# A gated two-layer cross-attention kernel on one core: first queries and scores pulled in front of the last projections, the pair work of each turn put together and shifted, another order at the end

## What is computed

```python
x = x + tanh(g_xattn[0]) * cosine_attention(layernorm(x), ctx)        # layer 0
x = x + tanh(g_ffn[0])   * ternary_ffn(layernorm(x))                  # layer 0
q = layer_norm(layernorm(x), g_norm) @ Wq                             # layer 1, attention
k, v = split(ctx @ Wkv)                                               # plus a null key and value
p = softmax(q @ k.T / 8)                                              # per head, 128 x 129
y = layer_norm((p @ v) @ Wout, g_out)
x = x + tanh(g_xattn[1]) * y
x = x + tanh(g_ffn[1])   * int8_ffn(layernorm(x))                     # layer 1, one global scale
```

## Time and profile before

| what | us |
|---|---|
| median of 3 runs | 317.86 (317.69 to 320.22) |
| the profiled execution | 317.06 |
| its span in the trace | 315.2 |
| busy: PE, DVE, ACT, POOL | 288.3, 249.9, 236.7, 158.0 |

### The profile page before, as it was taken

The page is one execution under the profiler, slowest core; times in us unless marked ns, Lnnn a source line. Parts: engine busy times, 40 slices in busy tenths (PEclk is TensorE's granted clock), DMA queues, the critical chain, the costliest instruction groups (busy, mean ns, idle before and its releaser), DMA issues.

```text
span 315.2 us, 7749 instructions
## 1 busy us (share of the span) xinstructions
PE 288.3 (91%) x2618; PEld 238.6 (76%) x2618; DVE 249.9 (79%) x730; ACT 236.7 (75%) x811; POOL 158.0 (50%) x225
## 2 busy tenths in 40 slices
PE   6788999999999898999999999999999997977775
PEld 6567768687776676899998998989989896842475
DVE  3798999999977436766878878898788988858875
ACT  3777696969899667899887889878898886429290
POOL 2124617252442104655587896868857585453200
PEclk9999999999999999999999999999999999999979
DMA  5741010001020000000000000000000000000004
GB/s 157 195 120 25 1 27 1 1 2 67 3 67 1 2 0 0 2 3 3 2 3 0 2 2 2 2 2 4 0 3 2 1 2 3 2 0 0 1 2 133
DMA packets 11478, 6.67 MB, mean 21 GB/s; under 512 B 3824, under 2 KB 10992, under 8 KB 11440
## 3 DMA queue, kind: packets, MB, share of 16 engines
q1 hardware_dynamic: 10560, 5.99, 6.7%
q10 hardware_dynamic: 880, 0.20, 0.3%
HBM read 5.14 MB, written 1.05 MB: 20 GB/s over the span
## 4 chain that ended last, share of the span: by engine, by line
PE 46%; DVE 22%; ACT 11%; POOL 9%; issue 7%; DMA 3%; SPq 2%; DVEq 0%; ACTq 0%; POOLq 0%
PE psum L1074 9%; DVE rmx L2029 6%; PE psum L1078 6%; PE psum L1202 5%; PE psum L1080 5%; PE psum L1079 5%; PE psum L1523 4%; ACT work L1005 4%; PE psum L1539 4%; POOL work L584 3%; PE psum L1648 3%; DVE work L2022 2%; DMA KT<-in_L_ffn_w_down 2%; DVE hgm L2228 2%; DVE den L2044 2%
## 5 line engine op out<-in xcount | busy, mean ns | idle before, releaser
L1005 ACT ACTIVATE work<-psum,nmx 128x128 f32<-128x128 f32 x208 | 74.2, 408 | 0.0
L584 POOL TENSOR_TENSOR work<-work,rden 128x512 f32<-128x512 f32 x51 | 53.1, 1043 | 40.9 <-DVE rden L2048 40.9
L1005 ACT ACTIVATION_READ_ACCUMULATOR work<-psum,nmx 128x1 f32 x208 | 51.6, 248 | 0.0
L1074 PE MATMUL psum<-ident,work 128*128 128x128 f32 (+2 forms) x328 | 47.1, 276 | 4.6 <-POOL work L584 2.1
L1074 PEld LDWEIGHTS psum<-ident,work 128*128 128x128 f32 (+2 forms) x328 | 36.8, 141 | 11.3 <-issue 2.7
L2029 DVE TENSOR_REDUCE rmx<-psum 128x8 f32<-128x1024 f32 x32 | 38.5, 1204 | 4.5 <-PE psum L1202 4.5
L1078 PE MATMUL psum<-split 128*128 128x256 f32 (+1 forms) x96 | 36.7, 383 | 3.0 <-ACT work L993 1.5
L1202 PE MATMUL psum<-KT,work 64*128 64x128 f32 x512 | 35.9, 283 | 2.0 <-ACT work L1005 1.2
L1202 PEld LDWEIGHTS psum<-KT,work 64*128 64x128 f32 x512 | 31.4, 187 | 6.5 <-issue 4.3
L2044 DVE SCALAR_TENSOR_TENSOR den<-null_exp,masked,key_sum 128x4 f32<-128x4 f32 x64 | 19.1, 299 | 18.9 <-ACT work L1005 13.0
L1080 PE MATMUL psum<-split 128*128 128x256 f32 (+1 forms) x96 | 30.6, 319 | 0.0
(11 more groups left out here) (216 smaller groups left out, 767.8 us busy)
## 6 DMA issues: line engine op xcount, KB each, us to landing
KT<-in_L_xattn_Wkv SPq DMA_DIRECT2D x2, 384.0 KB, 4.5
X<-in_x SPq DMA_DIRECT2D x1, 768.0 KB, 5.6
out_x<-X SPq DMA_DIRECT2D x3, 256.0 KB, 2.6
work<-in_ctx SPq DMA_DIRECT2D x3, 192.0 KB, 2.5
work<-in_L_xattn_Wq SPq DMA_DIRECT2D x1, 512.0 KB, 3.7
work<-in_L_xattn_Wout SPq DMA_DIRECT2D x1, 512.0 KB, 4.0
X<-in_x SPq DMA_DIRECT2D x1, 256.0 KB, 3.5
KT<-in_L_ffn_w_gate SPq DMA_DIRECT2D x1, 256.0 KB, 5.4
```

Source lines behind the costliest of these rows:

```text
L584: pool.tensor_tensor(sx_, sx_, bcast(rden[n % 2][:, :], S), ALU.mult).then_inc(p_ready.sem, 1)
L1005: ins = act.activation(Sx[n % 5][:, j, :], bank[2 * (r % 2) + j % 2][:, at * S:(at + 1) * S], ACT.Exp, bias=nmx[r % 2][:, col:col + 1], ac ...
L1074: return pe.transpose(dst, src, ident[0:m, 0:m])
```

## The change

- **Seam.** `q_first(0)` goes in front of `kv(60)` and `q_first(1)` behind `kv(61)`, into banks 5 and 6, with waits on those banks alone. `scores(0)` and `scores(1)` come right behind `kv(63)`; they now wait for the copies of chunks 0 to 62 and of one query chunk. `next_transposes(3)`, `q_first(2)` and `q_first(3)` follow them. On ACT the copies of the first two query chunks stand among those of the chunks 60 to 63, and those of the last two in turn 1, each behind the exponents of a unit.
- **Turns, DVE.** Both pair works stand between the second and the third denominator. The maxima of round 2M stand in front of the fourth denominator.
- **Turns, when pair work is done.** Statistics of the sum one round later (m = 4t + 14), aggregation and rstd one round later (15), normalised rows one round later (16 and 17), their maximum at 18. On POOL rstd of the sum thereby moves from the first half of an odd turn to its end, behind `y_affine`.
- **Drain.** DVE does the maxima of round 31 first and its copies in another order. POOL normalises all 64 units and does its pair work 32 behind unit 63. The steps of pairs 4 and 5 that had been done in turn 16 or before now stand among the last ones.
- 18 idle-filling matmuls in place of 22, and other banks for them.

```diff
-        X_STATS_AT, X_AGGR_AT, RSTD_X_AT, XN4_AT, GM_AT = 13, 14, 14, 15, 17
+        X_STATS_AT, X_AGGR_AT, RSTD_X_AT, XN4_AT, GM_AT = 14, 15, 15, 16, 18
...
             for M in range(NT + 1):
                 for k in range(2):
                     for n in range(4 * (M - 1) + 2 * k, 4 * (M - 1) + 2 * k + 2):
-                        if 0 <= n < NS - 1:
+                        if n >= 0:
                             normalise(n)
-                    pair_work(2 * M + k)
+                    if M < NT:
+                        pair_work(2 * M + k)
+            pair_work(2 * NT)
             rstd_x(NPAIR - 3)
...
-            for k in range(58, 64):
+            for k in range(58, 61):
                 kv_evac(k)
-            q_evac(0, bank[0])
-            q_evac(1, bank[1])
+            q_evac(0, bank[5])
+            kv_evac(61)
+            kv_evac(62)
+            q_evac(1, bank[6])
+            kv_evac(63)
             x_evac(3)
-            q_evac(2, bank[0])
-            q_evac(3, bank[1])
...
                     if q_round(2 * M + k):
                         q_round_evac(*q_round(2 * M + k))
+                    elif M == 1:
+                        q_evac(2 + k, bank[5 + k])
...
                 if hg == 0:
                     pe.wait_ge(wq_split.sem, wq_split.at(2))
                     pe.wait_ge(xs_ready.sem, xs_ready.at(1))
-                    pe.wait_ge(kv_out.sem, kv_out.at(0, NG))
-                    pe.wait_ge(cos_step.sem, cos_step.at(1, NG - 1))
-                    pe.wait_ge(third_in.sem, third_in.at(third(("u", NG - 1)) + 1))
+                if hg < 2:
+                    pe.wait_ge(hqT_ready.sem, hqT_ready.at(3 + hg, NG - 1))
...
                 if n == 0:
-                    pe.wait_ge(q_out.sem, q_out.at(4))
+                    pe.wait_ge(kv_out.sem, kv_out.at(NKV - 1, NG - 1))
+                    pe.wait_ge(cos_step.sem, cos_step.at(1, NG - 1))
...
             down(3, 3)
-            for k in range(60, 64):
-                kv(k)
-            q_first(0, bank[0])
-            q_first(1, bank[1])
-            next_transposes(3)
-            q_first(2, bank[0])
-            q_first(3, bank[1])
+            q_first(0, bank[5])
+            kv(60)
+            kv(61)
+            q_first(1, bank[6])
+            kv(62)
+            kv(63)
             scores(0)
             scores(1)
+            next_transposes(3)
+            q_first(2, bank[5])
+            q_first(3, bank[6])
...
-                    keep_clock_long(bank[5], 2)
+                    keep_clock_long(bank[4], 2)
...
-                    keep_clock_long(bank[5], 22)
+                    keep_clock_long(bank[4], 18)
...
             for M in range(NT + 1):
                 old, new = 4 * (M - 2), 4 * (M - 1)
+                if M == NT:
+                    maxima(2 * M - 1)
                 if old >= 0:
                     p_evac(old)
                     p_evac(old + 1)
+                if 0 < M < NT:
+                    maxima(2 * M - 1)
                 if new >= 0:
-                    maxima(2 * M - 1)
                     denominators(new)
                 if old >= 0:
                     p_evac(old + 2)
+                if M == NT:
+                    denominators(new + 1)
+                if old >= 0:
                     p_evac(old + 3)
-                if new >= 0:
+                if 0 < M < NT:
                     denominators(new + 1)
                 if M == NT:
                     p_evac(NS - 4)
-                pair_work(2 * M)
+                else:
+                    pair_work(2 * M)
+                    pair_work(2 * M + 1)
                 if new >= 0:
                     denominators(new + 2)
                 if M < NT:
-                    pair_work(2 * M + 1)
+                    maxima(2 * M)
                 if new >= 0:
                     denominators(new + 3)
-                if M < NT:
-                    maxima(2 * M)
-            last_normalise()
             p_evac(NS - 3)
             p_evac(NS - 2)
+            pair_work(2 * NT)
             pair_work(2 * NT + 1)
+            x_statistics(NPAIR - 3)
+            pair_max(NPAIR - 4)
             x_aggregate(NPAIR - 3)
```

More of the change, by code:

```diff
@@ L340, in flamingo_kernel @@
         vey_done, vex_done, rstdy_done, rstdx_done = (sig(n + "_done") for n in ("vey", "vex", "rstdy", "rstdx"))
-        p_last, pt_last, y_centred = sig("p_last"), sig("pt_last"), sig("y_centred")
+        pt_last, y_centred = sig("pt_last"), sig("y_centred")
         y_norm = sig("y_norm")
@@ L1489, in p_transposes @@
                 r, h = divmod(n, 2)
-                if n < NS - 1:
-                    pe.wait_ge(p_ready.sem, p_ready.at(n + 1))
-                else:
-                    pe.wait_ge(p_last.sem, p_last.at(1))
+                pe.wait_ge(p_ready.sem, p_ready.at(n + 1))
                 if n == NS - 4:
@@ L2063, in y_aggregate @@
                     dve.bn_aggr(mvy[:, bb, :], sty[:, bb, :]).then_inc(y_aggr.sem, 1)
-            def last_normalise():
-                n = NS - 1
-                b, hg = unit(n)
-                dve.wait_ge(rden_done.sem, rden_done.at(n + 1))
-                dve.tensor_tensor(Sx[n % 5], Sx[n % 5], bcast(rden[n % 2][:, :], S), ALU.mult).then_inc(p_last.sem, 1)
             def output_row(t, bb):
```

## The result

The changed kernel takes **315.37 us** (median of 14 runs, 314.70 to 319.19) against 317.78 for the kernel before (14 runs beside it). The ratio is 0.992, with an interval of 0.9892 to 0.9948: 2.4 us faster, where 6.6 were forecast.

What follows compares the result with a forecast made beforehand. No engine alone was taken to set the end; turns ran above PE's floor of 9.05 us. 317.06 - 4.2 (seam) - 0.3 (turns 3 to 5) - 3.0 (turns) + 0.9 (drain) = 310.5 profiled, 311.3 as median, range 307.5 to 315.5.

Steps and rivals of the forecast that it cites:

- Step 1, the seam: From last projection to turn 3: scores start at 109.35 instead of 113.04, 4.2 us gained, bounds 3.0 and 4.7.
- Step 2, the turns: Ten turns from turn 6 to turn 16: 94.2 against 97.21, 3.0 us gained, bounds 6.7 and -2.7.
- The copies out of PSUM start 0.1 later than now; hidden by 0.5.: In the turns: moving the fourth denominator behind the maxima delays DVE's copies by 0.1, with 0.5 to hide it.
- Most of that lies inside the wait for POOL in the odd turn: Maxima 1.2 late in even turns mostly cost nothing, as PE waits anyway; 0.4 for all turns, bounds 0 and 6.
- the signs of being right: Trace signs, among them turns 9 and 11 about 10.3 long, with PE idle before L1074 released by POOL L584.
- The denominator's move alone is hidden, with 1.0 to spare: In the turns: POOL normalises the fourth unit by 1.99 into the next turn; PE wants it at 2.97.
- even turns over 9.5: A sign of being wrong: even turns this long would show the port shared by DVE and POOL.
- Step 3, the drain: From turn 16 to the end: unit 60 normalised later and residual behind four units, 0.9 us lost, bounds -0.4 and 1.5.
- The seam's gain is swallowed: Rival: ACT's copies or `x_evac(3)` bind scores or second turn, leaving only the turns' gain; 315.5 us, chance 0.07.
- DVE and POOL hold each other up: Rival: late maxima add 1.2 in three or four turns, turns give nothing, drain costs 1.5; 314.9 us, chance 0.20.
- the two delays fall into the same wait of PE: Argument against the rival of DVE and POOL holding each other up, whose 1.2 comes on top in three or four turns.
- Slower: Rival: a POOL and DVE loop sets the pace, odd turns 12.0, even 9.6; 323.8 us, deciding from 20.5 a pair; chance 0.06.

Runs made afterwards that it cites:

- The square: Changed kernel with the fourth denominator behind or in front of the maxima, rstdx at 15 or 14: behind 315.37 and 310.66, in front 311.34 and 309.76 us.
- the last experiment: Changed kernel with a turn's fourth denominator moved behind DVE's first two copies of the next turn: 324.58 us, ratio 1.0214 to the kernel before.

## Why the prediction was right, and where it was wrong

**Step 1, the seam: right.** 4.05 for 4.2, first scores 109.10 for 109.35, turn 3 at 127.48 for 127.3. Its order of causes held as well: it had 2.8 from the seam's edit alone, which gave 2.9, and the maxima in front of the fourth denominator gave the rest. Turns 3 to 5 gave the 0.3 forecast (0.55 less the 0.25 of the ten turns).

**Step 2, the turns: the step that failed.** POOL's start (0.99 for 1.07), the time of rstdx (6.5 for 6.6) and the end of its stretch (13.2 for 13.61) were right. What was mis-sized is the lateness of the odd turns. In the sum stood 0.3, 1.3, 1.3, 0.4 and 0 for turns 7 to 15, and 0.4 for all hold-ups, together 3.7 over ten floors of 9.05. Measured were 0.9, 2.0, 2.0, 1.5 and 0.4, and 6.5 in all (96.95 - 90.5). Two sentences failed:
- "The copies out of PSUM start 0.1 later than now; hidden by 0.5." In turn 9 they start 5.45 behind the scores, in before 4.27 (189.77 and 185.50). In turn 7, where nothing waits for rstdx, 4.33; PE waits from about 3.8 on. The denominator was priced by its 0.35 alone, but behind the maxima it falls beside POOL's normalisation of the third unit and takes 1.07.
- "Most of that lies inside the wait for POOL in the odd turn": it does, in turn 9 (1.6 late by DVE, 1.5 by POOL), but not in turns 7 and 13, where POOL was forecast 0.3 and 0.4 late and PE waited for DVE's copy (0.41 and 0.87 idle in front of L1079). In all four long turns the releaser is DVE L2026, where the signs of being right named POOL L584. The wait also isn't one that runs beside the other: POOL's fourth unit waits for the late denominator, the two push each other.

"The denominator's move alone is hidden, with 1.0 to spare" held nearly (0.7 with rstdx early), and so it hid the point: the 1.0 to spare and the 0.99 of rstdx were spent from the same slack. The square shows it: 0.7 and 0.2 alone, 4.5 together. The forecast did have both in its sum of 13.2. It didn't ask what each would be without the other, and one number in the table turned out to decide 3.8 us of the turns. The sign that it gave for the port, "even turns over 9.5", didn't show either: even turns took 8.99, and what DVE lost beside POOL came out in the odd ones.

**Step 3, the drain: sign right, size off.** The term "0.9 lost" measured 2.2. The start of unit 60 was right (5.63 for 5.72). The residual behind unit 63, on which the step built its 0.9, costs 0.35 to 0.4. The fall of the clock behind PE's wait, which the step didn't have, costs 0.5; it is in three of the five traces with that wait, those of the changed kernel, of turns and drain without the seam (25.97) and of the last experiment (26.07), and not in the two others. The rest is the late fourth unit of the last turn. With the denominator in front of the maxima the drain is 24.04, only 0.2 over before, although the residual stands where the change put it; with rstdx early it is 24.42. PE's wait of 1.84 and the fall of the clock are gone in both.

**The rivals.** Nearest in number was *The seam's gain is swallowed*, 315.5 for 315.37, and that was luck: the seam gave its 4.05 in full. By mechanism it was *DVE and POOL hold each other up*: 314.9, with nothing gained in the ten turns (0.25 measured) and 1.5 lost in the drain (2.2 measured). What was held against it, "the two delays fall into the same wait of PE", was the mistake. *Slower* named a loop between POOL and DVE. In the changed kernel a pair of turns takes at most 20.05, under its 20.5. The last experiment passes that point with 21.5 for turns 8 and 9, and has an odd turn of 11.9 and an even one of 9.6 for the rival's 12.0 and 9.6. It is another kernel, so its 324.58 beside the rival's 323.8 is no test of that sum.

**What stays open.** Even the shortest ten turns of these runs, 92.44 and 92.46, are 1.9 over ten floors. In the kernel with rstdx and split PE shows only two idle rows of 0.15 there, and in the one with denominator and rstdx put back none, so what lengthens their turns isn't a wait that the trace names. And first scores start between 108.54 and 112.31 in the traces of the changed kernel and of those derived from it with the new seam, with 1.00 granted in the first 20 us at the early end and 0.81 to 0.83 at the late one. Why the clock falls there in some executions isn't known. It can move medians of 4 to 6 runs by 1 to 2 us; the length of the turns in a trace is the sharper measure, to its 0.5.

The fastest versions are two edits away from the change: rstdx at 14 with the split at 6 (309.54, 4 runs), or rstdx at 14 with the denominator in front (309.76, 6 runs), 8 us under before and 5.6 under the change. Their intervals don't tell them apart.

## What to carry to other kernels

When two edits each use up slack of the same wait, price all four combinations, not the sum and not each alone: here 0.7 and 0.2, hardly more than chance, became 4.5. A small instruction that another engine waits for is priced by what is queued behind it on both engines, and by its duration beside the neighbour it will now stand next to (0.22 alone, 1.07 there). And a move that is meant to help one stage is to be run without the rest: the seam alone was worth about as much as the whole change.

## What the runs showed of the hardware

Which of POOL's instructions hold DVE's up. A fourth denominator of 4 numbers a partition took 1.07 beside `normalise` (L584, TENSOR_TENSOR) and 0.70 beside the gain (L609, TENSOR_TENSOR, 184.54 to 185.26), each time ending with it. Beside `y_affine` (L603, TENSOR_SCALAR, 179.93 to 181.50) it took 0.27. Where `y_affine` alone ran beside it, it never took more than 0.34 in any trace of this case (86 of them); with nothing beside it, it takes 0.19 to 0.23. The maxima (1.19 to 1.23) and the copies out of PSUM (1.27) were the same beside everything. The Trainium skill ("SBUF — State Buffer", Who interferes with whom) has a shared pair of ports that VectorE takes for two SBUF inputs or in a two-port mode and never for a `tensor_reduce` on trn2; the rows of the maxima, of `nmx` and of the 1.07 agree, and the 0.27 beside a GpSimd instruction that reads SBUF doesn't follow from it.

The granted clock. Behind a wait of 1.84 PE was granted 0.50 from 263 to 265 in the changed kernel, that is 1.2 GHz of the levels 1.2 and 2.4, and so it was behind the same wait in the kernel without the seam and in the last experiment. Behind one of 1.84 in the kernel with the split moved, and one of 1.85 in that with the residual moved, it kept 1.00. The fall cost 0.5 of the drain. What told the executions apart isn't in these traces.
